# Transposes of the attention probabilities laid between the products of a matmul unit

## The reference

```python
nx = _ln(x, ln1_g, ln1_b)
q, k, v = heads(nx @ wq + bq), heads(nx @ wk + bk), heads(nx @ wv + bv)
bias = where(adj > 0, 0.1 * adj * adj, -inf)
attn = softmax(q @ k.T / sqrt(32) + bias)
x1 = x + (merge(attn @ v) @ wo + bo)
n2 = _ln(x1, ln2_g, ln2_b)
out = x1 + gelu(n2 @ w1 + b1) @ w2 + b2      # w1: 256x1024, w2: 1024x256
```

## Time and profile before

| | us |
|---|---|
| median of 3 runs | 1585.09 |
| lowest, highest | 1583.51, 1585.19 |
| the profiled execution | 1585.44 |
| its span in the profile | 1583.6 |
| PE busy | 1526.3 (96%) |
| ACT busy | 1149.1 (73%) |
| DVE busy | 1011.0 (64%) |

### The profile page before, as it was taken

One profiled execution on the slowest core, in us unless ns is written; L12 is line 12 of the kernel. 1 busy time (PEld: TensorE's weight loads), 2 busy tenths in 40 slices (PEclk: granted clock), 3 DMA queues, 4 the chain that ended last, 5 costly groups with the idle time before them and its releaser, 6 DMA issues.

```text
span 1583.6 us, 36063 instructions
## 1 busy us (share of the span) xinstructions
PE 1526.3 (96%) x12604; PEld 1297.7 (82%) x12604; DVE 1011.0 (64%) x2129; ACT 1149.1 (73%) x3335; POOL 486.9 (31%) x392
## 2 busy tenths in 40 slices
PE   6799999999999999999999999999999999999988
PEld 5578888888888888888888888888888888888777
DVE  4666666766666756666656666666666666666553
ACT  3777777777777777777777678777778777778772
POOL 3332333312333213333213333213333223333100
PEclk9999999999999999999999999999999999999999
DMA  3101110001111011110001111011100011100000
GB/s 127 41 2 34 35 33 30 9 28 34 35 34 32 7 31 33 33 33 30 8 31 34 36 32 33 5 34 33 33 30 22 16 34 34 33 30 14 5 15 27
DMA packets 55142, 46.69 MB, mean 29 GB/s; under 512 B 3344, under 2 KB 54800, under 8 KB 55056
## 3 DMA queue, kind: packets, MB, share of 16 engines
q1 hardware_dynamic: 55056, 45.38, 9.1%
HBM read 28.58 MB, written 16.78 MB: 29 GB/s over the span
## 4 chain that ended last, share of the span: by engine, by line
PE 74%; ACT 10%; DVE 10%; issue 6%; DVEq 0%; DMA 0%; POOL 0%; ACTq 0%; SPq 0%; POOLq 0%
PE work L330 17%; PE work L332 16%; PE work L331 15%; PE area L450 8%; PE turned L408 6%; ACT soft L626 5%; PE area L437 5%; DVE soft L788 4%; PE area L390 3%; DVE nmax L792 2%; PE turned L468 2%; DVE xt_lo L886 2%; ACT probt L617 2%; PE area L421 2%; ACT hid L680 1%
## 5 line engine op out<-in xcount | busy, mean ns | idle before, releaser
L626 ACT ACTIVATE soft<-soft,nmax 128x128 f32<-128x128 f32 x1024 | 396.2, 392 | 83.8 <-DVE nmax L792 83.7
L894 DVE TENSOR_TENSOR hid_parts<-hid,hid_parts 128x512 fp32r<-128x512 f32 x256 | 215.0, 851 | 142.5 <-ACT hid_parts L687 142.5
L330 PE MATMUL work<-w_hi,hid_parts 128*128 128x256 f32 x1024 | 294.9, 288 | 1.4 <-DVE res L905 1.0
L977 POOL TENSOR_TENSOR ve<-mv,eps 128x4 f32<-128x4 f32 x64 | 12.9, 202 | 904.7 <-DVE mv L852 473.7
L332 PE MATMUL work<-w_hi,hid_parts 128*128 128x256 f32 x1024 | 285.6, 279 | 0.0
L331 PE MATMUL work<-w_lo,hid_parts 128*128 128x256 f32 x1024 | 285.3, 279 | 0.0
L680 ACT ACTIVATE hid<-work,b_col 128x512 f32<-128x512 f32 x256 | 178.0, 695 | 73.1 <-PE work L332 69.7
L330 PE MATMUL work<-nt_hi,w_hi 128*128 128x512 f32 x512 | 224.2, 438 | 1.9 <-DVE nt_lo L886 1.7
L788 DVE TENSOR_TENSOR soft<-area,ebias 128x1024 f32<-128x1024 f32 x128 | 155.7, 1216 | 96.9 <-PE area L390 96.8
L332 PE MATMUL work<-nt_hi,w_lo 128*128 128x512 f32 x512 | 201.7, 394 | 0.0
L330 PEld LDWEIGHTS work<-w_hi,hid_parts 128*128 128x128 f32 x1024 | 191.9, 187 | 11.7 <-issue 5.9
(11 more groups left out here) (87 smaller groups left out, 3000.1 us busy)
## 6 DMA issues: line engine op xcount, KB each, us to landing
xin<-in_x SPq DMA_DIRECT2D x32, 512.0 KB, 4.0
out<-res SPq DMA_DIRECT2D x128, 128.0 KB, 1.7
adj_in<-in_adj SPq DMA_DIRECT2D x32, 256.0 KB, 4.1
w_raw<-in_L_gnn_w SPq DMA_DIRECT2D x1, 1024.0 KB, 8.1
soft<-in_L_gnn_w SPq DMA_DIRECT2D x1, 1024.0 KB, 10.4
wa_raw<-in_L_gnn_wq SPq DMA_DIRECT2D x1, 256.0 KB, 3.9
wa_raw<-in_L_gnn_wk SPq DMA_DIRECT2D x1, 256.0 KB, 4.3
wa_raw<-in_L_gnn_wv SPq DMA_DIRECT2D x1, 256.0 KB, 5.4
```

Source lines behind the costliest of these rows:

```text
L330: pe.matmul(o, lhs_hi, rhs_hi, start=first, stop=False)
L626: a = act.activation(soft[:, b % 2, h, :], soft[:, b % 2, h, :], ACT.Exp, bias=nmax[:, b % 2, h:h + 1], accum_out=rsum[:, b % 2, h:h + 1])
L894: dve.tensor_tensor(hid_lo[:, m, :], hid[:, m % 3, :], hid_hi[:, m, :].bitcast(F32), ALU.subtract).then_inc(hid_lo_ready, 1)
```

## The change

Three of the four turns of a step are no longer blocks of eight transposes. A new function `six` issues the six products of a unit and puts the transposes between them: heads 0 and 1 behind the first product, 2 and 3 behind the second, 4 and 5 behind the third, 6 behind the fourth, 7 behind the fifth, and then the sixth product. Turn 0 goes into query_key 0, turn 2 into query_key 3 and turn 3 into up 1. Turn 1 stays a block. Where a step has no such unit (at the ends of the pipeline), the turn is issued as a block. The waits of a turn go with its transposes. Nothing changes on the other engines.

```diff
@@ -392,22 +392,42 @@
                                        tile_position=(g * HD, 0))
                 mm.then_inc(scores_full, 1)
 
+            def turn_heads(step, b, heads):
+                if not step.has(0):
+                    return
+
+                for h in heads:
+                    half = h // 4
+                    if h == 0:
+                        if b == 0 and step.has(1):
+                            pe.wait_ge(taken["xt"], step.count(1, DC, DC - 1))
+                        if b == 3 and step.has(-1):
+                            pe.wait_ge(taken["nt"], step.count(-1, DC, DC - 1))
+                        if step.steady or step.n > 0 or b > 0:
+                            pe.wait_ge(turned_taken, step.upto(0, b - 1, 2))
+                    if h % 4 == 0:
+                        pe.wait_ge(prob_ready, step.upto(0, b, 2) - (1 - half))
+                    mm = pe.transpose(turned[:, half, (h % 4) * P:(h % 4 + 1) * P], soft[:, b % 2, h, :],
+                                      ident[:, :])
+                    if h % 4 == 3:
+                        mm.then_inc(turned_full, 1)
+
             def turn(step, b):
-                if not step.has(0):
-                    return
-
-                if b == 0 and step.has(1):
-                    pe.wait_ge(taken["xt"], step.count(1, DC, DC - 1))
-                if b == 3 and step.has(-1):
-                    pe.wait_ge(taken["nt"], step.count(-1, DC, DC - 1))
-                if step.steady or step.n > 0 or b > 0:
-                    pe.wait_ge(turned_taken, step.upto(0, b - 1, 2))
-                for half in range(2):
-                    pe.wait_ge(prob_ready, step.upto(0, b, 2) - (1 - half))
-                    for j in range(4):
-                        mm = pe.transpose(turned[:, half, j * P:(j + 1) * P],
-                                          soft[:, b % 2, half * 4 + j, :], ident[:, :])
-                    mm.then_inc(turned_full, 1)
+                turn_heads(step, b, range(H))
+
+            def six(step, b, o, lhs_hi, lhs_lo, rhs_hi, rhs_lo):
+
+                mm = pe.matmul(o, lhs_hi[0], rhs_hi[0], start=True, stop=False)
+                turn_heads(step, b, (0, 1))
+                mm = pe.matmul(o, lhs_hi[0], rhs_lo[0], start=False, stop=False)
+                turn_heads(step, b, (2, 3))
+                mm = pe.matmul(o, lhs_lo[0], rhs_hi[0], start=False, stop=False)
+                turn_heads(step, b, (4, 5))
+                mm = pe.matmul(o, lhs_hi[1], rhs_hi[1], start=False, stop=False)
+                turn_heads(step, b, (6,))
+                mm = pe.matmul(o, lhs_hi[1], rhs_lo[1], start=False, stop=False)
+                turn_heads(step, b, (7,))
+                return pe.matmul(o, lhs_lo[1], rhs_hi[1], start=False, stop=True)
 
             def spread(step, b):
                 if not step.has(0):
@@ -483,8 +503,10 @@
                                    c == 0, c == DC - 1)
                 mm.then_inc(full["v"], 1)
 
-            def query_key(step, m):
+            def query_key(step, m, turning=None):
                 if not step.has(1):
+                    if turning is not None:
+                        turn(step, turning)
                     return
                 free(step, "qk", m)
                 if not step.steady and step.n == -1:
@@ -494,13 +516,20 @@
                 if m == 0:
                     pe.wait_ge(taken["xt"], step.count(1, DC, DC - 1))
                 w, cols = m // DC, slice((m % DC) * P, (m % DC + 1) * P)
-                for c in range(DC):
-                    mm = three(work[:, bank_of("qk", m), :], wa_hi[:, w, c, cols], wa_lo[:, w, c, cols],
-                               xt_hi[:, c, :], xt_lo[:, c, :], c == 0, c == DC - 1)
+                if turning is not None:
+                    mm = six(step, turning, work[:, bank_of("qk", m), :],
+                             [wa_hi[:, w, c, cols] for c in range(DC)], [wa_lo[:, w, c, cols] for c in range(DC)],
+                             [xt_hi[:, c, :] for c in range(DC)], [xt_lo[:, c, :] for c in range(DC)])
+                else:
+                    for c in range(DC):
+                        mm = three(work[:, bank_of("qk", m), :], wa_hi[:, w, c, cols], wa_lo[:, w, c, cols],
+                                   xt_hi[:, c, :], xt_lo[:, c, :], c == 0, c == DC - 1)
                 mm.then_inc(full["qk"], 1)
 
-            def up(step, m):
+            def up(step, m, turning=None):
                 if not step.has(-1):
+                    if turning is not None:
+                        turn(step, turning)
                     return
                 free(step, "up", m)
 
@@ -509,9 +538,14 @@
                 if not step.steady and step.n == 1 and m == 0:
                     pe.wait_ge(lo_made, 5)
                 cols = slice(m * P, (m + 1) * P)
-                for c in range(DC):
-                    mm = three(work[:, bank_of("up", m), :], w1_hi[:, c, cols], w1_lo[:, c, cols],
-                               nt_hi[:, c, :], nt_lo[:, c, :], c == 0, c == DC - 1)
+                if turning is not None:
+                    mm = six(step, turning, work[:, bank_of("up", m), :],
+                             [w1_hi[:, c, cols] for c in range(DC)], [w1_lo[:, c, cols] for c in range(DC)],
+                             [nt_hi[:, c, :] for c in range(DC)], [nt_lo[:, c, :] for c in range(DC)])
+                else:
+                    for c in range(DC):
+                        mm = three(work[:, bank_of("up", m), :], w1_hi[:, c, cols], w1_lo[:, c, cols],
+                                   nt_hi[:, c, :], nt_lo[:, c, :], c == 0, c == DC - 1)
                 mm.then_inc(full["up"], 1)
 
             def down(step, b):
@@ -540,8 +574,7 @@
                 score(step, 1)
                 down(step, 1)
                 down(step, 2)
-                turn(step, 0)
-                query_key(step, 0)
+                query_key(step, 0, turning=0)
                 spread(step, 0)
                 turn(step, 1)
                 mix(step, 0)
@@ -554,8 +587,7 @@
                 project_out(step, 0)
                 query_key(step, 2)
                 score(step, 3)
-                query_key(step, 3)
-                turn(step, 2)
+                query_key(step, 3, turning=2)
                 values(step, 0)
                 flip(step, "nt", 0)
                 flip(step, "nt", 1)
@@ -565,8 +597,7 @@
                 project_out(step, 1)
 
                 up(step, 0)
-                turn(step, 3)
-                up(step, 1)
+                up(step, 1, turning=3)
                 up(step, 2)
                 spread(step, 3)
                 up(step, 3)
```

More of the change, by code:

```diff
@@ L393, in score @@
                 mm.then_inc(scores_full, 1)
-            def turn(step, b):
+            def turn_heads(step, b, heads):
                 if not step.has(0):
                     return
-                if b == 0 and step.has(1):
-                    pe.wait_ge(taken["xt"], step.count(1, DC, DC - 1))
-                if b == 3 and step.has(-1):
-                    pe.wait_ge(taken["nt"], step.count(-1, DC, DC - 1))
-                if step.steady or step.n > 0 or b > 0:
-                    pe.wait_ge(turned_taken, step.upto(0, b - 1, 2))
-                for half in range(2):
-                    pe.wait_ge(prob_ready, step.upto(0, b, 2) - (1 - half))
-                    for j in range(4):
-                        mm = pe.transpose(turned[:, half, j * P:(j + 1) * P],
-                                          soft[:, b % 2, half * 4 + j, :], ident[:, :])
-                    mm.then_inc(turned_full, 1)
+                for h in heads:
[13 more added lines that the diff above has]
+                        mm.then_inc(turned_full, 1)
@@ new lines, in turn @@
+            def turn(step, b):
+                turn_heads(step, b, range(H))
[11 more added lines that the diff above has]
+                return pe.matmul(o, lhs_lo[1], rhs_hi[1], start=False, stop=True)
```

## The result

| | us |
|---|---|
| median of 4 runs (lowest, highest) | 1614.11 (1610.02, 1616.65) |
| the kernel before, same comparison | 1584.3 |
| ratio, 95% interval | 1.0186 (1.0173 to 1.020) |
| the profiled execution, its span | 1613.64, 1611.5 |

A forecast was written before the change was run, and what follows sets the result against it. TensorE, busy 96% of the span, was taken to set the time by its order of work. Transposes 1.8, turn 2 15.9 and turn 0 3.0 summed to +20.7 us, given as 1605.5 us, range 1590 to 1612.

The forecast's parts named there:

- A transpose costs 0.11 us in any place: Transposes between products: each is set by its stationary load, so order does not matter; +1.8 us over about 92 units.
- Rival A: Transposes between products: their loads disappear under the products, turn 3 giving -12.7 us; net -7, 1578 us; 6%.
- rival C: Units with transposes: breaking an accumulation into six pieces costs in itself, 29 us on top, 1635 us; 6%.
- Turn 2: Query/key unit 3: ScalarE copies that unit before the turned probabilities, so the nhat flips wait 0.53 us, 30 times: +15.9 us.
- part 1: The transposes themselves, in all three units: +0.02 us a unit, about 92 units, +1.8 us (0.9 to 4.6).
- Turn 0 in the steady steps: Query/key unit 0: nothing in 24 ordinary steps, 0.50 us in each of 6 where turn 1 had not waited: +3.0 us.
- The cover: Before turn 1: ScalarE reaches turn 0's copies late anyway, so the later last transpose is in time by 0.1 us.
- Part 3: Turn 0 between the products of query/key unit 0: +3.0 us (0 to 5), from 6 steps at 0.50 us.
- Rival B: The 0.53 us wait ahead of the nhat flips is given back later or made up by ScalarE: 1587 us; 8%.

The follow-up runs named there:

- turn 3 alone: The changed kernel with turns 0 and 2 as blocks again, only turn 3 between products: 1586.54 us, 1.0010 of the kernel before.
- covered version: The changed kernel with ScalarE copying turn 2 first, blocks in steps 0 and 1, and 9 down-projection unit 3 products ahead of turn 1: 1572.0 us.
- block counterpart: The kernel before, all turns as blocks, with the first 9 of 24 products of down-projection unit 3 moved ahead of turn 1: 1570.2 us, 0.9922.
- start blocks: The changed kernel with turns 0 and 2 as blocks in steps 0 and 1: 1606.59 us, 1.0150 of the kernel before.
- turn 2 alone: The changed kernel with turns 0 and 3 as blocks again, only turn 2 between products: 1603.41 us, 1.0117 of the kernel before.

## Why the prediction came out as it did

1. **A transpose costs 0.11 us in any place: right.** Units with transposes take 2.27 to 2.28 us (2.26 before), with turn 2's at 2.39 for the reason told above, turn 3 alone is +0.1%, and the covered version is within 2 us of its block counterpart. Rival A (loads hidden, -12 us for turn 3 alone) and rival C (a switch costs, +9) are both excluded by these runs. The reading of the Trainium skill ("TensorE: Matmul & The Clock Gate", its opening table) as several loads ahead does not hold in this kernel.
2. **Turn 2: right in mechanism, a little small.** Predicted 15.9 us, with part 1's share 16.5; alone it measured about 18.5. The wait by distance of starts is 0.56 instead of 0.53, and the flips behind it take longer: 1.09 us for eight with a wait ahead, 1.04 in the earlier trace rows. This restart stood in the earlier trace rows already (1.09 behind a wait, 1.03 without) and was not counted: 30 x 0.05 = 1.5 us.
3. **Turn 0 in the steady steps: right.** The cover held in the ordinary steps and failed where turn 1 had not waited; predicted 3.0, with part 1's share 3.6, measured 4.6 (2.7 to 6.5).
4. **Turn 0 in steps 0 and 1: the step that failed.** Part 3 took its ordinary step from the steady part, counted 24 steps like it and 6 without cover, and has no term for the start. There the products that were drawn in between the transposes had been the filling of the next wait. The wait became 2.96 us in one piece, and behind it the granted clock was half, by the mean clock in three of the four runs of the changed kernel for long. This costs 7.5 us in the median (start blocks against the full change); the prediction had nothing for it. With the blocks put back in two steps the kernel runs at 1606.6, against the 1605.5 forecast, or 23.1 over the kernel before that ran beside it, against 20.4. What is left of the sum is close, but turn 2 and the steady turn 0 were each 1 to 2 us too small. The measured parts (18.5, 4.6, 1.6 for turn 3, 7.5) add up to 32 against 29.8, which their intervals allow. In the one run at 0.996, 1610.0, the whole would have lain within the range; that there are such runs was not foreseen either.
5. **Rival B, delay given back: wrong**, as argued: turn 2's wait alone shows in full in the time.

What stays open: why the same program at the start falls into the longer half-clock stretches in some runs and not in others. That it is turn 0 at the start is shown by the runs with blocks there and by turn 2 alone; what ends a half-clock stretch early or late is not. The few loop-edge waits, which also move from run to run, were not tried.

## What to carry to other kernels

Before moving work between other work, ask for each consumer which of its engine's earlier list entries now ends last: an engine that copies in order makes the early half of a result useless when its place is behind the late one. Count the stationary loads, not the streams, before expecting that small matmuls vanish between large ones. Treat pipeline fill as its own case: products used up early leave one long wait, and here the clock behind it cost several us while the wait itself cost none. Work put where TensorE waits in every step gave 0.8% for one wait and 1.2% for two.

## What the runs showed of the hardware that was not expected

- At the half clock a block of eight transposes takes 1.97 us against 1.09 at the full one, both behind a wait: the distance of two transposes, which at full clock is set by the stationary loads (0.11), doubles to 0.21. The load side shows it too: eight loads span 1.57 us at half clock and 0.86 at full (the rows below). The loads are not a fixed time that the slower clock leaves alone.
- A chain of transposes behind a wait takes 0.05 us longer than the same chain behind running work (1.09 against 1.03 or 1.04 us).
- A break of the accumulation in a PSUM bank by transposes into another bank, five times in a unit, has no price beyond 0.01 to 0.02 us.

The load rows, first of the changed kernel at half clock, then of the one before at full:

```profile
47.50 1.57 PEld L410 LDWEIGHTS turned<-ident,soft 128*128 128x128 f32 x8 [3.20 <-ACT probt L648]
```

```profile
48.10 0.86 PEld L408 LDWEIGHTS turned<-ident,soft 128*128 128x128 f32 x8 [1.15 <-ACT probt L617]
```
